# Turned values times step sizes, first group: from VectorE to ScalarE by token tile and head

## The reference

```
hid  = silu(causal_conv(proj_hid))              # 128 heads of 64
dt   = softplus(dt + dt_bias)                   # one step size per token and head
hid_dt = hid * dt[..., None]                    # the product that is moved
Y_diag = einsum(M, hid_dt);  Y_off = einsum(C, states(hid_dt), decay)
y = (Y_diag + Y_off + D * hid) * silu(gate)
out = rmsnorm_by_group(y) @ out_proj.T
```

## Time and profile before

| what | value |
|---|---|
| median of 3 runs | 792.56 us (792.37 to 793.35) |
| the profiled execution, its own time | 794.21 us |
| its span, first to last instruction | 792.4 us |
| busy: PE, DVE, POOL, ACT | 97%, 89%, 75%, 69% of the span |
| mean granted TensorE clock | 0.999 |

### The profile page before, as it was taken

The page is one execution under the profiler, slowest core; times in us unless marked ns, Lnnn a source line. Parts: engine busy times, 40 slices in busy tenths (PEclk is TensorE's granted clock), DMA queues, the critical chain, the costliest instruction groups (busy, mean ns, idle before and its releaser), DMA issues.

```text
span 792.4 us, 14394 instructions
## 1 busy us (share of the span) xinstructions
PE 771.5 (97%) x4192; PEld 607.2 (77%) x4194; DVE 706.3 (89%) x906; ACT 549.8 (69%) x1145; POOL 593.8 (75%) x488
## 2 busy tenths in 40 slices
PE   8989999999999999999999999999999999999987
PEld 7867787788778777787788777887787777878743
DVE  5999999989898989999899988899899989999774
ACT  4687776767766766766767766677767677788464
POOL 6478877787797887788787887788777976788512
PEclk9999999999999999999999999999999999999999
DMA  7463344434434434343434434543444345541001
GB/s 219 162 236 118 122 160 148 145 134 160 149 117 158 159 132 143 148 159 124 148 138 172 159 108 144 172 157 98 146 167 172 131 161 185 183 164 42 13 1 53
DMA packets 43793, 111.12 MB, mean 140 GB/s; under 512 B 5748, under 2 KB 6644, under 8 KB 43764
## 3 DMA queue, kind: packets, MB, share of 16 engines
q1 hardware_dynamic: 43444, 109.71, 40.7%
q0 software_dynamic: 320, 1.05, 0.3%
HBM read 109.30 MB, written 1.44 MB: 140 GB/s over the span
## 4 chain that ended last, share of the span: by engine, by line
PE 88%; DVE 7%; issue 2%; ACT 1%; POOL 1%; DMA 1%; POOLq 0%; SPq 0%; DVEq 0%
PE ps_in L1370 17%; PE ps_in L1372 15%; PE ps_in L1371 15%; PE ps_y L1484 8%; PE ps_o L1370 7%; PE ps_o L1372 7%; PE ps_o L1371 7%; PE ps_t L1446 3%; PE ps_y L1487 3%; DVE hid L1049 1%; PE ps_t L1496 1%; PE ps_t L1458 1%; DVE stats L1251 1%; DMA res<-in_x 1%; PE ps_o L1689 1%
## 5 line engine op out<-in xcount | busy, mean ns | idle before, releaser
L535 POOL TENSOR_TENSOR w_lo<-raw,w_hi 128x512 fp32r<-128x512 f32 x144 | 233.5, 1642 | 102.3 <-ACT w_hi L655 101.0
L1370 PE MATMUL ps_in<-h_hi,w_hi 128*128 128x512 f32 x560 | 226.2, 404 | 0.7 <-DVE gate L1068 0.7
L1372 PE MATMUL ps_in<-h_hi,w_lo 128*128 128x512 f32 x560 | 219.1, 391 | 0.0
L1371 PE MATMUL ps_in<-h_lo,w_hi 128*128 128x512 f32 x560 | 217.9, 389 | 0.0
L710 ACT ACTIVATE e<-e,nag 128x256 f32<-128x256 f32 (+1 forms) x512 | 183.6, 444 | 4.1 <-DVE nag L1119 4.1
L1049 DVE SCALAR_TENSOR_TENSOR hid<-ps_in,curc,hid 128x510 f32<-128x510 f32 x183 | 136.1, 744 | 4.4
L1370 PEld LDWEIGHTS ps_in<-h_hi,w_hi 128*128 128x128 f32 x560 | 105.0, 187 | 31.1 <-issue 10.1
L566 POOL TENSOR_TENSOR e<-e,gm 128x512 f32<-128x512 f32 x64 | 99.5, 1555 | 32.4 <-DVE gm L1093 27.6
L1372 PEld LDWEIGHTS ps_in<-h_hi,w_lo 128*128 128x128 f32 x560 | 105.1, 188 | 23.3
L1371 PEld LDWEIGHTS ps_in<-h_lo,w_hi 128*128 128x128 f32 x560 | 105.3, 188 | 20.2
L675 ACT ACTIVATE hid<-ps_in,curc 128x512 f32<-128x512 f32 x61 | 47.4, 777 | 102.7 <-PE ps_in L1372 102.6
(11 more groups left out here) (235 smaller groups left out, 1169.2 us busy)
## 6 DMA issues: line engine op xcount, KB each, us to landing
e<-acs_rows SPq DMA_DIRECT2D x64, 768.0 KB, 4.5
raw<-in_w_in SPq DMA_DIRECT2D x144, 256.0 KB, 4.8
rawo<-in_w_out SPq DMA_DIRECT2D x64, 256.0 KB, 4.1
craw<-in_ctx SPq DMA_DIRECT2D x8, 256.0 KB, 4.7
res<-in_x SPq DMA_DIRECT2D x4, 256.0 KB, 3.6
acs_rows<-z SPq DMA_DIRECT2D x3, 128.0 KB, 2.0
rawo<-in_w_dt SPq DMA_DIRECT2D x1, 256.0 KB, 4.8
perm_row<-in_perm SPq DMA_DIRECT2D x1, 256.0 KB, 3.4
```

Of the source, the lines that this page charges most:

```text
L535: pool.tensor_tensor(w_lo[:, slot, :], raw[:, slot, :], w_hi[:, slot, :].bitcast(F32), ALU.subtract).then_inc(s_lo, 1)
L1370: pe.matmul(dst, lh, rh, start=first, stop=False)
L1371: pe.matmul(dst, lh, rl, start=False, stop=False)
L1372: return pe.matmul(dst, ll, rh, start=False, stop=last)
```

## The change

In steps 4 to 7 of the first group VectorE no longer calls `turned`. ScalarE computes the same values with eight ACTIVATE instructions, one for each token tile and head (128 partitions x 64 columns out of `ps_t`, scale taken from one column of `dtg`), right behind the gate tanh and ahead of the step's casts. The semaphores that are waited for and the count given at the end are those of `turned`; the wait for the group's step sizes (`s_curg`) is new on ScalarE.

```
+            def turned_by_head(q):
+                act.wait_ge(s_t, q + 1)
+                act.wait_ge(s_curg, 2)
+                act.wait_ge(s_y, q - 1)
+                for c in range(TT):
+                    for hh in range(2):
+                        h = 2 * q + hh
+                        last = act.activation(hdt[:, q % 2, c, hh * HD:(hh + 1) * HD],
+                                              ps_t[:, c * P + hh * HD:c * P + (hh + 1) * HD], ACT.Copy,
+                                              scale=dtg[:, c, h:h + 1])
+                last.then_inc(s_tf, 1)
...
                 gate_tanh(*lagged(n, t, 2))
+                if is_first(n) and t >= FIRST_STEPS:
+                    turned_by_head(t - 1)
                 for tile in tiles:
                     cast_in(*tile)
...
-                turned(*lagged(n, t, 1))
+                if not (is_first(n) and t >= FIRST_STEPS):
+                    turned(*lagged(n, t, 1))
                 taps(n, ("h", t))
```

## The result

The changed kernel takes 804.5 us (median of 4 runs, 804.15 to 804.94) beside 792.95 us for the kernel before (4 runs, 792.37 to 793.43): a ratio of 1.0145, with a 95% interval of 1.0134 to 1.0157. The forecast was 797.4 with a range of 794.2 to 801. The direction is right, the size is not: 11.5 us were lost where 4.8 were forecast. The profiled execution took 804.67 us, its span 802.9 us and not 792.4.

What follows compares the result with a forecast made beforehand. Bound: TensorE and VectorE, both full in the first group. Late ScalarE casts and tap 0 make VectorE 4.0 us late by step 7, plus 0.8 beside GpSimd: 792.56 + 4.8 = 797.4 us, range 794.2 to 801.

Steps and rivals of the forecast that it cites:

- the sum's 4.0 + 0.8: VectorE 4.0 us late at the taps of h 7, plus 0.8 beside a busy GpSimd: 4.8 us in all.
- The bound: First group: TensorE and VectorE both full, so a microsecond TensorE loses there is found again in the end time.
- the price of the block: ScalarE's eight small ACTIVATEs cost 1.6 us a step, with bounds of 0.69 and 3.1 us.
- the place of the wait and what is queued behind it: ScalarE waits for the transposes of t-1; casts, tanh of B or C, tap 0 and exponentials queue behind.
- the first two links: Steps 5 and 6: taps of h 5 at 78.8, 3.3 us late; taps of h 6 at 89.2, 3.2 late.
- Step 4's lead of 0.7: Step 4: later gate cast keeps GpSimd's split off VectorE's work; transposes of tile 4 end at 73.8, not 74.54.
- The expected signs: Small ACTIVATEs behind transposes, VectorE idle, TensorE waiting for step 6's outputs and second-group scores, old trace shifted behind 130 us.
- the path of step 6: Bank of h 6 free at 91.4, then three TensorE tiles of 2.73 us; transposes of tile 6 at 99.6, 2.2 later.
- from there to 126: Taps of h 7 to 126 us: VectorE slowed beside busy GpSimd, 0.8 us taken, bounds nothing and 3.3.
- the coupling at the scores: Second group's scores: VectorE's delay feeds TensorE's wait for z, 1.2 us before, so TensorE's delay equals VectorE's.
- The relief that the prediction expected for later stretches: Later stretches: GpSimd's work may equally move off VectorE's; given as the reason for taking 0.8 us, not 3.3.
- The rival that was called deeper: ScalarE's small instructions cost 3.1 us a step, three links grow by 1.5 each: 801.9 us; chance 12%.

Runs made afterwards that it cites:

- Step 4 alone: The change applied in step 4 only, steps 5 to 7 as in the kernel before: 792.86 us, ratio 1.0001.
- run that was kept busy in both waits: Changed kernel with small identity matmuls in TensorE's two long waits and the second group's steps written out on TensorE: 801.92 us, ratio 1.0104.
- run with GpSimd held: Changed kernel with GpSimd held in step 7, ahead of its masks, until VectorE's z_low of tile 5 is done: 802.71 us, ratio 1.0122.
- run of step 5 alone: The change applied in step 5 only, steps 4, 6 and 7 as in the kernel before: 797.1 us, ratio 1.0068.
- run with the wait alone: Kernel before, with ScalarE waiting for the transposes of t-1 where the change puts its block; VectorE still does the product: 804.48 us, ratio 1.0146.
- run with the written-out turn: Changed kernel with the second group's steps written out on TensorE in place of the loop's first turn, without small matmuls: 805.04 us, ratio 1.0133.

## Why the prediction was wrong in size

The steps, in the order of the prediction (us from the start of the span):

| mark | before | forecast | after |
|---|---|---|---|
| block of eight ACTIVATEs, us | none | 1.6 | 1.59 |
| taps of h 5 | 75.50 | 78.8 | 78.82 |
| taps of h 6 | 85.95 | 89.2 | 88.86 |
| transposes of tile 6 | 97.40 | 99.6 | 101.32 |
| taps of h 7 | 100.71 | 104.7 | 106.49 |
| end of the decay product of tile 6 | 108.40 | 113.2 | 118.34 |
| outputs of that tile | 108.94 | | 118.55 |

The forecast for the decay product is the old end, 107.17 + 1.23, and the sum's 4.0 + 0.8.

**Right.** The bound (two full engines with no play between them), the price of the block, the place of the wait and what is queued behind it, and the first two links, within 0.4 us. That the taps of h 5 came out to 0.02 us is luck: tap 0, which was to release them, is done at 77.64 + 0.82 = 78.46, and they start when VectorE's own silu of B ahead of them, slow at 1.59 us, is through. Step 4's lead of 0.7 was there as well: the transposes of tile 4 start at 72.81 and not at 73.94, of which 0.3 is an earlier start of the whole stretch. Step 4 alone changed nothing in the end time, so this small lead was rightly left without a price at the end. The expected signs were all there but one: behind 130 us the trace is the old one, shifted by one amount, and TensorE is idle 0.8 us in all from 140 to 745, as the busy time of that stretch shows:

```profile
140.00:745.00 605.00, 604.19 (x3277) 481.70 (x3275) 550.53 (x670) 429.94 (x914) 485.23 (x389) 1.00 0.43 145
```

**Wrong, first: the path of step 6, and a term that was missing.** The prediction let TensorE wait some 2 us for the outputs of step 6 and gave the wait no price of its own, since the bank of h 6 was taken to hold TensorE longer. The bank held nothing: the taps of h 6 had left it at 91.1, and behind the outputs TensorE ran four tiles without a pause, from 90.30 to 101.3. The other part is the clock. The prediction did not see that the granted clock falls to 0.50 in such a wait; the outputs then took 2.76 and not 1.45 us. Without these 1.3 us the four tiles would have ended at 100.0, still 0.7 later than by the bank, 91.1 + 8.2 = 99.3 with the three tiles that the prediction put behind it. The run that was kept busy in both waits bears this out, in TensorE's timeline from the outputs to the transposes of tile 6:

```profile
89.42 0.65 PE L1505 MATMUL ps_y<-e,hdt 128*64 128x256 f32 x4
...
101.89 0.60 PE L1463 MATMUL ps_t<-ident,hid 128*128 128x128 f32 x4
```

At a granted clock of 1.00 this takes 12.47 us, with the change 101.32 - 87.54 = 13.78. Behind the second wait the clock cost 1.3 us again on the outputs and 4.28 - 2.85 = 1.4 on the gate tile: 4.0 us together. The trace before had not shown it: through its waits of up to 1.6 us the clock stayed at 1.00.

**Wrong, second: the term "from there to 126" was too small.** It took 0.8 us for VectorE beside a busy GpSimd, with 3.3 as the upper bound from three instructions. Measured from the taps of h 7 to the end of the decay product, it is 4.2 us. silu grew by 1.77 - 0.68 = 1.1, z_low by 1.0, and three instructions that were not on the list by 1.0, 1.0 and 0.8 (the two small ones and the decay product), while 0.7 us of idle time that VectorE had before went away. The mechanism was right, and the run with GpSimd held shows it; the choice near the lower bound was wrong, and the bound itself counted too few instructions.

**Wrong, third: the coupling at the scores.** The prediction carried VectorE's delay to the wait for z at the second group's scores. This wait is no longer there. TensorE stood for 5.78 us for the outputs of tile 6 while VectorE went on. The relief that the prediction expected for later stretches came there: the next silu and z_low of VectorE take 0.68 and 0.75 us (123.06 and 124.02), where they took 1.78 each before. Soon VectorE waits for TensorE, as its timeline in the changed kernel shows:

```profile
131.76 0.69 DVE L1091 TENSOR_TENSOR hdt<-ps_t,dtg 128x512 f32<-128x512 f32 x1 [2.18 <-PE ps_t L1462]
```

It is not the half clock that did this: in the run that was kept busy in both waits the wait at the scores is gone as well, and VectorE waits 2.14 us at the same place. It gave back 1.2 us.

The sum as measured: the outputs of tile 6 start 118.55 - 108.94 = 9.6 us late, the clock behind them costs 2.7, the wait at the scores and smaller ones that are gone give back some 1.7, in all 10.6, beside 10.5 between the two spans. The medians are 11.5 apart because the profiled execution of the kernel before was a long one.

The rival that was called deeper came nearer to the time, with 801.9, by a wrong cause: the small ACTIVATEs cost 1.6 us a step and not 3.1.

The Trainium skill (SBUF — State Buffer, Who interferes with whom) would have put the second term at its upper bound, and that would have been nearer; the 1.28 us of an instruction on one row of 128 elements, 0.27 before, fits its rule that the later of the two waits for the whole of the other's instruction. The Trainium skill (TensorE: Matmul & The Clock Gate, What's actually happening) says that an idle TensorE goes back to half its clock. The changed kernel's trace agrees, with 0.50 granted behind the waits of 2.9 and 5.8 us; behind 2.93 us in the run of step 5 alone and 3.3 us in the run with the wait alone it stayed at 1.00. A price for that belonged into the sum, at least as a bound, as soon as a new wait of TensorE stood in it.

## What to carry to other kernels

When work is moved to an engine with idle time, the place in that engine's queue decides, not its load: a wait put ahead of instructions that others are fed from costs the whole chain behind them, while the same work at the end of the step, where its input is long there, was free. A new wait of a full TensorE can be dearer than its length, because the clock may fall in it; and a late engine meets other neighbours, so each of its instructions is to be priced beside a busy GpSimd and not by its last duration.

## What was not expected of the hardware

The same wait of 1.6 us, ahead of the outputs of tile 2, brings the half clock in some runs and not in others. TensorE's timeline from the transposes of tile 3 through those outputs, to the transposes of tile 4, first of the changed kernel and then of the run with the written-out turn:

```profile
57.97 0.66 PE L1462 MATMUL ps_t<-ident,hid 128*128 128x128 f32 x4 [0.40 <-DVE hid L1073]
...
60.89 0.63 PE L1500 MATMUL ps_y<-e,hdt 128*64 128x256 f32 x4
...
72.81 0.60 PE L1462 MATMUL ps_t<-ident,hid 128*128 128x128 f32 x4
```

```profile
57.26 0.66 PE L1462 MATMUL ps_t<-ident,hid 128*128 128x128 f32 x4 [0.45 <-DVE hid L1073]
...
60.18 1.10 PE L1500 MATMUL ps_y<-e,hdt 128*64 128x256 f32 x4
...
73.57 0.60 PE L1462 MATMUL ps_t<-ident,hid 128*128 128x128 f32 x4
```

The code up to there is the same. The second half of the outputs takes 0.63 us in the one and 1.10 in the other, and from the transposes of tile 3 to those of tile 4 pass 14.84 and 16.31 us. The granted clock from 61 to 63 us is 1.00 in the one and 0.50 in the other, so 1.5 us go to the clock. On the other side, a wait of 3.3 us in the run with the wait alone left the outputs behind it at full speed, in 1.45 us, and one of 2.93 us in the run of step 5 alone as well, where the 2.90 us of the changed kernel halved the clock. The mean granted clock of the kernel before scatters too, from 0.996 to 1.000 over seven runs of 792.28 to 794.04 us, though there the times do not follow it. In the run with the wait alone they do: 801.57 us at 0.996, 803.56 at 0.991, 805.39 and 806.03 at 0.988. What decides when the clock falls is left open here.
